# Attention inside a fused layer: weighted sums issued between score batches instead of after them

## The reference

```python
q = jnp.einsum('bsd,hde->bshe', x, W_Q) + b_Q
k = jnp.einsum('bsd,hde->bshe', x, W_K) + b_K
v = jnp.einsum('bsd,hde->bshe', x, W_V) + b_V
scores = jnp.einsum('bqhe,bkhe->bhqk', q, k) / jnp.sqrt(jnp.float32(D_HEAD))
scores = jnp.where(causal, scores, jnp.float32(-jnp.inf))
z = jnp.einsum('bhqk,bkhe->bqhe', jax.nn.softmax(scores, axis=-1), v)
x = _layernorm(x + jnp.einsum('bqhe,hed->bqd', z, W_O) + b_O)
hidden = fwht(jax.nn.silu(x @ W1.T) * (x @ W3.T))
x = _layernorm(x + hidden @ W2.T)
```

## Time and profile before

| what | value |
|---|---|
| timed runs | 8311.65 us median of 3 (8249.62 to 8895.34) |
| profiled execution | 8240.26 us, span 8238.7 us (slowest core, core 2) |
| spans of the 8 cores | 8189.7 to 8238.7 us |
| mean granted TensorE clock | 0.862 to 0.866 of full speed |

### The profile page before, as it was taken

One profiled execution on the slowest core, in us unless ns is written; L12 is line 12 of the kernel. 1 busy time (PEld: TensorE's weight loads), 2 busy tenths in 40 slices (PEclk: granted clock), 3 DMA queues, 4 the chain that ended last, 5 costly groups with the idle time before them and its releaser, 6 DMA issues. The chain is left out here.

```text
span 8238.7 us, 71476 instructions; the slowest of 8 cores (8189.7 to 8238.7 us)
## 1 busy us (share of the span) xinstructions
PE 5470.2 (66%) x27240; PEld 2625.8 (32%) x27648; DVE 1430.3 (17%) x2379; ACT 1010.6 (12%) x676; POOL 593.2 (7%) x776
## 2 busy tenths in 40 slices
PE   0023347667585757667547488888888888588687
PEld 0001114334353434344323233333333333233233
DVE  2024522221222222221214000000000000000101
ACT  0000002130303121121301011111111111000000
POOL 0001101010000001010000000000000000011011
PEclk9999998778686878778779799999999999899898
DMA  9985558273645647282454411111111110888886
GB/s 308 211 167 106 105 128 176 81 155 107 125 140 98 171 99 160 92 164 96 100 136 151 86 45 39 46 39 46 46 39 46 39 46 23 257 284 282 285 284 243
DMA packets 601221, 1081.68 MB, mean 131 GB/s; under 512 B 264128, under 2 KB 346048, under 8 KB 584384
## 3 DMA queue, kind: packets, MB, share of 16 engines
q0 software_dynamic: 236016, 538.01, 28.3%
q1 hardware_dynamic: 331024, 377.56, 16.2%
q10 hardware_dynamic: 33856, 161.51, 6.2%
HBM read 934.38 MB, written 234.88 MB: 142 GB/s over the span
## 5 line engine op out<-in xcount | busy, mean ns | idle before, releaser
L773 PE MATMUL psum<-Y_fm,W1b 128*128 128x512 bf16 x4016 | 1105.0, 434 | 306.8 <-DVEq L104 172.9
L898 PE MATMUL psum<-W2pb,HHc 128*128 128x512 bf16 x4014 | 918.9, 384 | 277.7 <-DMA W2pb<-w2p 231.9
L523 PE MATMUL psum<-Q,K 128*128 128x512 bf16 x1232 | 528.6, 575 | 705.5 <-ACTq L104 655.9
L778 PE MATMUL psum<-Y_fm,W3b 128*128 128x512 bf16 x4012 | 919.4, 379 | 4.4
L532 ACT ACTIVATE PT<-psum,expb,scl 128x2048 bf16<-128x2048 f32 x320 | 658.3, 2057 | 2142.0 <-PEq L104 2141.9
L266 PE MATMUL psum<-w2i,h64b 64*64 64x512 bf16 x512 | 240.9, 624 | 872.0 <-DVEq L104 853.7
L773 PEld LDWEIGHTS psum<-Y_fm,W1b 128*128 128x128 bf16 x4096 | 436.1, 109 | 956.3 <-issue 615.7
L898 PEld LDWEIGHTS psum<-W2pb,HHc 128*128 128x128 bf16 x4096 | 395.4, 99 | 801.2 <-issue 360.6
L789 DVE TENSOR_TENSOR h_sb<-psum,tmp_f 128x1024 bf16<-128x1024 f32 x128 | 156.8, 1225 | 2317.5 <-ACTq L104 2317.5
L778 PEld LDWEIGHTS psum<-Y_fm,W3b 128*128 128x128 bf16 x4096 | 400.5, 98 | 483.5
L454 PE MATMUL psum<-xcol,WKb 128*128 128x512 bf16 x1984 | 459.7, 391 | 117.1 <-DMA xcol<-xbf 85.3
(11 more groups left out here) (63 smaller groups left out, 1957.3 us busy)
## 6 DMA issues: line engine op xcount, KB each, us to landing
xcol<-xbf POOLq DMA_DIRECT2D x64, 2048.0 KB, 9.9
W2pb<-w2p POOLq DMA_DIRECT2D x256, 512.0 KB, 7.6
W2pb<-w2p SPq DMA_DIRECT2D x256, 512.0 KB, 5.5
xcol<-xof POOLq DMA_DIRECT2D x32, 2048.0 KB, 25.1
w2i<-w2t POOLq DMA_DIRECT2D x128, 256.0 KB, 4.2
xf_sb<-x_batch SPq DMA_DIRECT2D x16, 2048.0 KB, 36.6
w2p<-w2o ACTq DMA_DIRECT2D x128, 256.0 KB, 3.1
w13s<-w1t POOLq DMA_DIRECT2D x64, 512.0 KB, 7.6
```

The lines of the kernel that those rows point to most:

```text
L523: q.pe.append(lambda e, h=h, j=j, s=s, bank=bank: e.matmul(pb[bank][:], K2[:, h * S + j * 128:h * S + (j + 1) * 128], Q2[:, h * T + s * 51 ...
L773: q.pe.append(lambda e, wpar=wpar, c=c, tq=tq: e.matmul(pb[tq % 2][:], W1b[wpar][:, c * 128:(c + 1) * 128], Y_fm[:, c * T + tq * 512:c * T ...
L778: q.pe.append(lambda e, wpar=wpar, c=c, tq=tq: e.matmul(pb[2 + tq % 2][:], W3b[wpar][:, c * 128:(c + 1) * 128], Y_fm[:, c * T + tq * 512:c ...
L898: q.pe.append(lambda e, i=i, ts2=ts2, dc=dc, bank=bank, par=par, wb=wb: e.matmul(pb[bank][:], HHc[par][:, i * 256 + ts2 * 128:i * 256 + (t ...
```

## The change

The weighted sums of slot `s` are no longer issued as one block behind the scores of slot `s`+1. `av_unit_list` makes a list of them with their waits, and `emit_av_units` issues some of them after each batch of scores of slot `s`+1: 9 behind each batch of slot 1, 11 of slot 2, 13 of slot 3. What is left after the last batch, and all of slot 3's, follows as a block. The units of a slot begin with two waits, for the slot's last exp and for its mask; the waits ahead of the last 8 tiles of each quarter are gone. The code that takes z out (reciprocal, scale, transpose) comes with the last unit, which is now inside `emit_scores` of the next slot, ahead of that slot's masks. `emit_scores` also begins with a wait for the exp total of the slot before, which the first banks wait for anyway. Matmuls, exps, masks and transfers keep their number and shape.

```diff
+                        def av_unit_list(state):
+                            s, exp_total, mk, nj = state
+                            units = [('w', (SEM("s_exp"), exp_total)), ('w', (SEM("s_mask"), mk))]
+                            jorder = list(range(nj))
+                            for q4 in range(4):
+                                if tokZ[q4] is not None:
+                                    units.append(('w', tokZ[q4]))
+                                for ji, j in enumerate(jorder):
+                                    units.append(('m', s, j, q4, ji, nj))
+                            units.append(('d', s))
+                            return units
+
+                        def emit_av_units(units, n):
+                            cnt = 0
+                            while units and cnt < n:
+                                u = units[0]
...
+                                else:
+                                    s_ = u[1]
+                                    av = DI(q.pe, SEM("s_av"))
+                                    W(q.dve, SEM("s_av"), av)
+                                    for q4 in range(4):
...
-                        def emit_scores(s):
+                        def emit_scores(s, av_units):
                             nj = LIM[s] // 128
                             exp_base = SEM("s_exp").n
+                            W(q.pe, SEM("s_exp"), exp_base)
+                            per_batch = 12 if not av_units else max(6, (len([u for u in av_units if u[0] == 'm']) * 4) // nj + 1)
...
                                     DI(q.act, SEM("s_exp"))
+                                    av_units = emit_av_units(av_units, per_batch)
...
-                                    if j == nj - NMASK or (nj == NMASK and ji == 0):
-                                        W(q.pe, SEM("s_mask"), mk)
...
+                        av_units = []
                         for s in range(NSLOT):
-                            st = emit_scores(s)
-                            if prev is not None:
-                                emit_av(prev)
+                            st, av_units = emit_scores(s, av_units)
+                            av_units = emit_av_units(av_units, 1 << 30)
+                            av_units = av_unit_list(st)
                             prev = st
-                        emit_av(prev)
+                        emit_av_units(av_units, 1 << 30)
```

More of the change, by code:

```diff
@@ L509, in build @@
                             W(q.sp, *zfw_tok[hg % 2])
-                        slot_state = []
-                        def emit_scores(s):
+                        def av_unit_list(state):
[9 more added lines that the diff above has]
+                            return units
@@ new lines, in emit_av_units @@
+                        def emit_av_units(units, n):
+                            cnt = 0
+                            while units and cnt < n:
+                                u = units[0]
+                                if u[0] == 'w':
+                                    W(q.pe, *u[1])
+                                    units.pop(0)
+                                elif u[0] == 'm':
+                                    _, s_, j, q4, ji, nj = u
+                                    q.pe.append(lambda e, j=j, q4=q4, h=h, zb=4 + q4, ji=ji, nj=nj, sp2=s_ % 2: e.matmul(
+                                        pb[zb][:, 0:129],
+                                        PT[sp2][:, j * 512 + q4 * 128: j * 512 + (q4 + 1) * 128],
+                                        V2e[:, j * 258 + h * 129: j * 258 + (h + 1) * 129],
+                                        start=(ji == 0), stop=(ji == nj - 1)))
+                                    units.pop(0)
+                                    cnt += 1
+                                else:
[3 more added lines that the diff above has]
+                                    for q4 in range(4):
+                                        zb = 4 + q4
+                                        if ztr_tok[q4] is not None:
+                                            W(q.dve, *ztr_tok[q4])
+                                        q.dve.append(lambda e, q4=q4, zb=zb: e.reciprocal(
+                                            rz_sb[:, q4:q4 + 1], pb[zb][:, 128:129]))
+                                        DR(q.dve)
+                                        q.dve.append(lambda e, q4=q4, zb=zb: e.tensor_scalar(
+                                            out=z_sb[q4][:], in0=pb[zb][:, 0:128],
+                                            scalar1=rz_sb[:, q4:q4 + 1], scalar2=None, op0=ALU.mult))
+                                        zev = DI(q.dve, SEM("s_zev"))
+                                        tokZ[q4] = (SEM("s_zev"), zev)
+                                        W(q.sp, SEM("s_zev"), zev)
+                                        col = (s_ * 4 + q4) * 128
+                                        ztr_tok[q4] = DMA(q.sp, f"s_ztr{q4}",
+                                                          lambda e, q4=q4, col=col, h=h: e.dma_start_transpose(
+                                                              out=zTst[h][:, col:col + 128], in_=z_sb[q4][:]))
+                                    units.pop(0)
+                            return units
@@ L538, in emit_scores @@
                                 tokA[b] = (SEM("s_exp"), exp_total)
-                            exp_base2 = exp_base
                             for j in range(nj - NMASK, nj):
-                                W(q.dve, SEM("s_exp"), exp_base2 + j // 4 + 1)
+                                W(q.dve, SEM("s_exp"), exp_base + j // 4 + 1)
                                 q.dve.append(lambda e, j=j, s=s, sp2=s % 2: e.scalar_tensor_tensor(
@@ L587, in build @@
+                            return (s, exp_total, mk, nj), av_units
                         prev = None
+                        av_units = []
                         for s in range(NSLOT):
-                            st = emit_scores(s)
-                            if prev is not None:
-                                emit_av(prev)
+                            st, av_units = emit_scores(s, av_units)
+                            av_units = emit_av_units(av_units, 1 << 30)
+                            av_units = av_unit_list(st)
```

## The result

| | before | after |
|---|---|---|
| timed runs, median of 10 | 8501.0 us | 8579.2 us |
| lowest | 8248.5 | 8465.6 |
| ratio to before | 1 | 1.0281, 95% interval 1.0223 to 1.034 |

The change makes the kernel 2.8% slower, about 232 us on 8248.5.

The account below looks back on a forecast made before the run. It took PE and ACT alternating in the attention as the bound, 4.26 us a batch. Per group 2 x 101.0 - 200.9 + 29.3 = 30.4 us more, 243 in eight; on 8240.3 that gave 8483, put at 8500, range 8400 to 8620.

Parts of the forecast that it names:

- What bounds the stage: Attention: score batches and exps alternate at 4.26 us a batch, with nothing else of PE in the 2.40 us holes.
- (a): Weighted sums of slots 0 to 2 run under the exps: 17.3 us a head, 277 us over 16 heads.
- (b): New wait: PE needs the exp total and all of the mask before a slot's first weighted sum; score batches stand behind.
- (c): DVE at slot ends: z (3.2 us) now precedes the next masks (5.1 us); with (b) it eats (a)'s gain.
- The clock: Attention batches followed by sums: taken at 3.42 us each after slot 1, slot 1's at 4.26; both levels in the range.
- the sum: An undisturbed attention head takes 101.0 us; with the stall, 243 us more over eight groups, giving 8483.
- The rival with the low clock: Attention: as forecast, but batches mixed with sums stay at 1.2 GHz: 8627; chance 0.18 (or something between).
- (d): Each group's first head: z of slot 1 waits for transposes behind SP's conversion stores, stalling PE 29.3 us, until 86.8.
- Transposes as fast as other DMAs: Skill's rule for z's transposes: at most 4.0 us, making the sum 27 us less; forecast used the row's 7.4.
- No stall: Rival, SP's queue: slot 0's transposes land by 49 us into the group; 9 us in all, 8249; chance 0.08.
- Full overlap: Rival, attention: the mask wait falls entirely under the running exp, all of (a) comes, 7963; chance 0.04.
- the last step, from the sum to 8500: Whole kernel: from 8483, with the timed median 8311.65 at 0.9% and lowest 8249.6 at 0.1% above profiled, to 8500.

Follow-up runs that it names:

- both repairs: Changed kernel with eight z_sb buffers and masks ahead of z on DVE: a group 184.0 to 184.8 us, lowest runs 8078.4 and 8108.5, no ratio formed.
- the seam filled: On both repairs, slot 3's sums of a group's first head go behind slot 0's batches of its second: ratio 0.9725 to the kernel before.
- eight buffers: Changed kernel with eight z_sb buffers instead of four, DVE's order as changed: ratio 1.0026 to the kernel before.

## Why the prediction was right, and where not

*What bounds the stage: right.* Score batches and exps took turns; the holes were there and were filled. PE's wait for ACT fell by 245 us.

*(a) the gain: right in kind.* No kernel here had all of it, the 17.3 us a head. With both repairs 16 to 17 us a group came of it, 8 a head; the waits left at the ends of slots, 1.52 + 2.36 + 5.35 = 9.2 us, are about what is missing. The 27 us a group with the seam filled hold a gain that was not in (a), since slot 3's sums move too.

*(b) and (c) the slot ends: right.* The forecast put the sums of slots 1, 2 and 3 at 31.6, 57.5 and 90.7 us into a head that does not stall; in the second heads of core 4 they start at 29.5, 56.0 and 89.6 in the mean. It took such a head for 101.0; second heads measured 100.2. Of the waits that it named, 4 to 7 us, those of slots 1 and 2 are 4.5 to 5.8, but slot 3's is 8.5 to 9.0: there no score batch of a next slot stands in front of it.

*The clock: right for slot 3, in part for slot 2.* Rows of after, core 4: us, busy us of PE, PEld, DVE, ACT, POOL, then the granted clock.

```profile
2926.90:2937.00 10.10, 7.17 (x35) 3.69 (x35) 0.00 (x0) 5.62 (x3) 0.00 (x0) 0.55 0.85 155
3007.70:3028.00 20.30, 11.01 (x100) 6.73 (x102) 0.00 (x0) 12.34 (x6) 0.00 (x0) 1.00 0.71 219
```

Behind the slot 1 batches with nine sums the clock is mostly at its lower level (0.55 in the mean), and they stay at 4.26 us, as the sum had it. Among batches with 13 sums it is at 1.00, 2.4 GHz, and they come every 3.4 us. Slot 2 lies between: the sum took 3.42 for all its batches, but the first behind each wait takes 4.2 to 4.3, and 23 of 64 take over 3.9. The rival with the low clock fell; its own figure, 8627, would have lain outside the range that was said to hold most of it. The rule for dense matmuls (the Trainium skill, "TensorE: Matmul & The Clock Gate", section "Loop structure matters more than you think"), by which slot 1 would have been fast too, is not borne out for slot 1 here and agrees with slot 3.

*(d) the stall: right.* PE went on at 84.7 us in the mean of core 4's groups and 86.2 over the four cores of its die, where 86.8 was forecast; its removal by eight buffers gave 8 x (228.6 - 203.1) = 204 us back, where 8 x 29.3 = 234 was the term. The term was some 7 to 15% too large: a first head is 128.4 - 102.8 = 25.6 us longer than without the stall by these two cores, 129.7 - 102.3 = 27.4 by the means of the die's four cores and of the eight with the buffers. I had also said that the wait would read 25 to 30 us. It reads 27.6 to 35.9, since the row holds the ordinary wait of that slot's end, 5.7 us, as well.

*Transposes as fast as other DMAs: not behind the stores.* First transpose issued at 2986.04, DVE released at 2995.43, 9.4 us. The Trainium skill, "Advanced Engine Details and Errata", section "X-Bar Transpose (TRN2)", has them as fast as regular ones. With the row I went by, 7.4, I was nearer.

*The rivals.* "No stall" would have needed the transposes by 49 us into the group; moving half of the stores agrees with that: with the last of them out at about 26 us there is no stall, and the heads are within 2.2 us of those of before. "Full overlap" needed the masks ahead of z, and with them there the heads fell below those of before.

*What failed: the last step, from the sum to 8500.* The sum itself held: 243 us on the profiled execution's 8240.3, that is 8483 and 2.9%, where the ratio says 2.8%, 232 us, and the runs of the changed kernel that it is formed from took 8465.6 to 8548.0. The step behind it took the median of three runs before, 8311.65, for a level that the changed kernel could be set against, and put the forecast at 8500, only 188 us above that median. It was no such level: with ten runs the same unchanged kernel's median was 8501.0, 189 us higher, and that of the changed one 8579.2. The two medians differ by 78 us, where 188 stood in the forecast. That 8579.2 lies inside 8400 to 8620 is luck: the upper part of the range stood for the low clock, which did not come. A forecast of a difference has to stand on the same level as what it is compared with. The mechanism, its place and its size do not depend on this step.

## What to carry to other kernels

When work is slid into an engine's idle time, list what the moved code takes along: here the evacuation of z moved with the last matmul, ahead of the masks on DVE, and the masks were what the next piece of work waited for. A wait that costs nothing (DVE's 20 us for the transposes before) is only as harmless as what stands behind it in the list and when that is due; look for such idle times on engines that the change reorders, and follow them to the queue that causes them, which here was a third engine's. Repairing the two waits turned a change that cost 2.8% into one that gains some 1.7% by its lowest runs, and 2.8% where the sums are carried over the seam of two heads as well.

## What the runs showed of the hardware that was not expected

In one and the same head of the changed kernel the clock was 0.55 in the mean where nine sums stand behind each batch (2926.9 to 2937.0) and 1.00 where thirteen do (3007.7 to 3028.0). It would be easy to read from this that the number of sums decides. The version with the filled seam shows that it is not so simple. Its slot 1 has nine sums behind each batch in both heads of a group; in the first head it comes behind two batches alone, in the second behind the 128 sums carried over the seam. Rows of core 5, fifth group: a piece of nine in either head, then the stretches from the second or first batch of the slot to its last.

```profile
2713.60 1.15 PE L566 MATMUL psum<-V2e,PT 128*128 128x129 bf16 x9
2796.10 0.69 PE L566 MATMUL psum<-V2e,PT 128*128 128x129 bf16 x9
```

```profile
2711.66:2720.18 8.52, 6.03 (x27) 2.79 (x27) 0.05 (x1) 4.11 (x2) 0.71 (x1) 0.55 0.99 177
2791.58:2801.84 10.26, 5.29 (x39) 2.74 (x40) 2.81 (x11) 6.17 (x3) 0.00 (x0) 1.00 1.23 284
```

The same work runs at 0.55 with a batch every 4.26 us where it found the clock low, and at 1.00 with a batch every 3.42 us where it found it high; it is so in all eight groups of this core. Thirteen sums behind each batch did bring the clock up from a low start: it was 0.52 in the stall ahead of them (2968.5 to 3004.0). So what runs ahead of a stretch counts beside the size of its pieces, and a piece of thirteen at the high level (0.91 us) costs less than one of nine at the low (1.15). No run here varied the size of the pieces alone.

And a small transpose of 32 KB that follows a train of 512 KB stores on one queue took 7.4 and 9.4 us to release DVE, against a median of 2.3 us to landing over the attention.
